# ScalarE fetches one tile of 64 row by row in pass L0 as well, and the second edge table reaches VectorE through PSUM

## What is computed

```python
h = jnp.maximum(_layernorm(x, axis=-1), 0.0)
x = x + _L0_gnn_ref(h, src, dst, edge_weight, L0_gnn_eps)       # (1+eps)*h + segment_sum(h[src]*edge_weight, dst)
h = jnp.maximum(_layernorm(x, axis=-1), 0.0)
x = x + _L1_gnn_ref(h, edge_index, edge_attr_64, edge_attr_64_n2, ...)
#   edge_weight = jnp.sum(z * edge_attr, axis=1); then 3 times:
#   agg = segment_sum(edge_weight[:, None] * (h @ conv_weight[i])[src], dst); h = gru_cell(agg, h, ...)
h = jnp.maximum(_layernorm(x, axis=-1), 0.0)
x = x + _L2_gnn_ref(h, edge_index, edge_type_16, ...)           # relation weights, attention
h = jnp.maximum(_layernorm(x, axis=-1), 0.0)
x = x + _L3_gnn_ref(h, edge_index, L3_gnn_W, L3_gnn_b)          # mean over edges, sorted by source
```

## Time and profile before

| | us |
|---|---|
| median of 3 runs | 6450.01 |
| lowest, highest | 6447.16, 6452.57 |
| profiled execution, its own time | 6448.79 |
| its span in the trace | 6446.7 |

### The profile page before, as it was taken

The page is one execution under the profiler, slowest core; times in us unless marked ns, Lnnn a source line. Parts: engine busy times, 40 slices in busy tenths (PEclk is TensorE's granted clock), DMA queues, the critical chain, the costliest instruction groups (busy, mean ns, idle before and its releaser), DMA issues.

```text
span 6446.7 us, 121607 instructions
## 1 busy us (share of the span) xinstructions
PE 3474.1 (54%) x13756; PEld 2716.5 (42%) x13756; DVE 3860.5 (60%) x14060; ACT 630.0 (10%) x1422; POOL 4692.6 (73%) x4970
## 2 busy tenths in 40 slices
PE   3444445666667555555655554695454444444444
PEld 3333334444444444554444444343343333333334
DVE  6767666666666676667677774454454444444445
ACT  1000002000001000000200000143333333000000
POOL 6777776777774677777777777675777776777775
PEclk6555556555556677667867775696555555555555
DMA  5333342222222222222222222263222222222222
GB/s 140 110 111 109 108 111 77 58 60 58 60 58 67 58 59 59 60 59 56 68 60 59 59 60 59 85 226 116 54 53 54 54 54 56 56 56 56 56 56 59
DMA packets 281533, 472.60 MB, mean 73 GB/s; under 512 B 103535, under 2 KB 178670, under 8 KB 274463
## 3 DMA queue, kind: packets, MB, share of 16 engines
q0 software_dynamic: 155024, 303.69, 18.6%
q1 hardware_dynamic: 89755, 94.70, 4.5%
q10 hardware_dynamic: 35956, 66.36, 3.0%
HBM read 379.46 MB, written 86.91 MB: 72 GB/s over the span
## 4 chain that ended last, share of the span: by engine, by line
POOL 35%; issue 20%; SPq 15%; DMA 14%; PE 10%; DVE 4%; ACT 1%; DVEq 1%; POOLq 0%; ACTq 0%
POOL G L731 34%; SPq L592 12%; DMA G<-h_rows,ix_src 10%; PE ps L835 10%; SPq L584 3%; DMA G<-h_rows 1%; DMA G<-t_rows,pos 1%; DMA t_rows<-G 1%; DVE HNA L1306 1%; PE ps L897 0%; DVEq L1295 0%; SPq L605 0%; ACT gate L1957 0%; DVE M L1286 0%; DVE bst L1223 0%
## 5 line engine op out<-in xcount | busy, mean ns | idle before, releaser
L731 POOL DMA_INDIRECT G<-h_rows,ix_src x3824 | 3632.5, 950 | 1273.9 <-issue 1017.4
L835 PE MATMUL ps<-G,M 128*128 x10000 | 2546.9, 420 | 2806.8 <-SPq L605 1904.6
L835 PEld LDWEIGHTS ps<-G,M 128*128 128x128 f32 x10000 | 2154.7, 308 | 3265.5 <-issue 3260.4
L1306 DVE TENSOR_TENSOR HNA<-HNA,ps 128x128 f32 (+1 forms) x3328 | 958.2, 288 | 1259.0 <-PE ps L835 1238.3
L1286 DVE TENSOR_SCALAR M<-irow,rel,w_l 128x128 f32<-128x128 f32 x3328 | 1205.7, 364 | 177.5 <-issue 170.7
L731 POOL DMA_INDIRECT G<-t_rows,pos x770 | 736.1, 956 | 261.3 <-issue 225.3
L1306 DVE TENSOR_TENSOR HTA<-HTA,ps 128x129 f32 x840 | 243.5, 290 | 502.0 <-PE ps L835 492.7
L835 PE MATMUL ps<-sorting 128*128 128x128 f32 x1568 | 419.1, 362 | 0.0
L1996 ACT ACTIVATE G<-G,pk 128x128 f32<-128x128 f32 x782 | 311.8, 402 | 673.0 <-DMA G<-t_rows,pos 671.7
L1306 DVE TENSOR_TENSOR X<-X,ps 128x128 f32 x832 | 239.5, 288 | 230.0 <-PE ps L835 218.0
L835 PEld LDWEIGHTS ps<-sorting 128*128 128x128 f32 x1568 | 352.6, 277 | 0.0
(11 more groups left out here) (274 smaller groups left out, 2069.8 us busy)
## 6 DMA issues: line engine op xcount, KB each, us to landing
G<-h_rows SPq DMA_DIRECT2D x7680, 0.5 KB
G<-h_rows ACTq DMA_DIRECT2D x4608, 0.5 KB
G<-h_rows,ix_src POOLq DMA_INDIRECT x3824
t_rows<-G SPq DMA_DIRECT2D x49, 1024.0 KB, 4.3
HTA<-in_edge_attr_n ACTq DMA_DIRECT2D x50, 500.0 KB
HTA<-in_edge_attr ACTq DMA_DIRECT2D x50, 500.0 KB
G<-t_rows SPq DMA_DIRECT2D x1536, 0.5 KB
G<-t_rows,pos POOLq DMA_INDIRECT x770
```

The costliest lines, as they stand in the source:

```text
L731: return nc.gpsimd.indirect_dma_start(to, None, table, bass.IndirectOffsetOnAxis(ap=ix, axis=0))
L835: return nc.tensor.matmul(dst, lhsT, rhs, start=start, stop=stop, skip_group_check=True)
L1306: V.tensor_tensor(to, to, ps[:, u % SLOTS, 0:n], ALU.add).then_inc(s_add, 1)
```

## The change

In pass L0 too, ACT fetches the 63rd tile of each 64, twelve tiles of 128 rows; POOL leaves these out. ACT does its loads of the edge tables between the rows, by a list of steps written out in the code (`edges_due`), and in the same places it copies the second table's chunk to PSUM, banks 4 and 5 or 6 and 7, two instructions of 512 columns. DVE multiplies from there: two instructions of 512 columns with one operand in SBUF and one in PSUM, where it had four of 256 with both in SBUF. It waits for ACT's copy (`s_ewp`) where it waited for the load (`s_ewl`). The semaphores of the row by row tiles are now shared by two passes each, and one wait is added in DVE's setup.

```diff
-EW_PIECE = 4
+EW_PIECE = EW_C // 2
...
-ACT_PASSES = (PASS_L1 + 1, PASS_L1 + 2, PASS_L3)
+ACT_PASSES = (PASS_L0, PASS_L1 + 1, PASS_L1 + 2, PASS_L3)
...
-        s_row = [[sem(f"s_row{k}_{q}") for q in range(2)] for k in range(3 + LAYERS)]
-        s_rowa = {k: [sem(f"s_rowa{k}_{q}") for q in range(2)] for k in ACT_PASSES}
+        s_row = [[sem(f"s_row{k}_{q}") for q in range(2)] for k in range((3 + LAYERS) // 2)]
+        s_rowa = [[sem(f"s_rowa{k}_{q}") for q in range(2)] for k in range((3 + LAYERS) // 2)]
...
             def ew_chunk(c, q, turn):
-                dve.wait_ge(s_ewl[q], 32 * (turn + 1))
-                for d in range(0, EW_C, EW_PIECE):
-                    to = za[:, q, 0, d:d + EW_PIECE, :]
-                    ins = V.tensor_tensor(to, to, za[:, q, 1, d:d + EW_PIECE, :], ALU.mult)
+                dve.wait_ge(s_ewp[q], turn + 1)
+                for h in range(2):
+                    to = za[:, q, 0, h * EW_PIECE:(h + 1) * EW_PIECE, :].rearrange("p c d -> p (c d)")
+                    ins = V.tensor_tensor(to, to, ps[0:EW_P, 4 + 2 * q + h, :], ALU.mult)
                 link(ins)
...
-            V.tensor_copy(wc[:], ps[:, 4:4 + LAYERS, 0:3 * D])
+            link(V.tensor_copy(wc[:], ps[:, 4:4 + LAYERS, 0:3 * D]))
...
+            act.wait_ge(s_ones, 16 * 2 * ROW_PARTS)
             for q in range(2):
                 ew_load(q, q)
...
-            with act.Fori(0, EW_CHUNKS // 2 - 1) as i:
-                for q in range(2):
-                    act.wait_ge(s_ewc, 2 * i + q + 1)
-                    ew_load(2 * i + 2 + q, q)
+
+            def ew_second(q, turn):
+                act.wait_ge(s_ewl[q], 32 * (turn + 1))
+                for h in range(2):
+                    ins = A.copy(ps[0:EW_P, 4 + 2 * q + h, :],
+                                 za[:, q, 1, h * EW_PIECE:(h + 1) * EW_PIECE, :].rearrange("p c d -> p (c d)"))
+                ins.then_inc(s_ewp[q], 1)
...
+            def slot_free(k, j):
+
+                act.wait_ge(s_mm, max(k * S + (j - 2) * RING + BY_ACT + BLK, 1))
+
+            loaded, copied = [2], [0]
+
+            def edges_due(step):
+                while loaded[0] < EW_CHUNKS and 16 * loaded[0] + 12 <= step:
+                    c = loaded[0]
+                    act.wait_ge(s_ewc, c - 1)
+                    ew_load(c, c % 2)
+                    loaded[0] += 1
+                while copied[0] < min(loaded[0], EW_CHUNKS) and max(16 * copied[0] + 26, 36) <= step:
+                    c = copied[0]
+                    if c == 0:
+                        act.wait_ge(s_eix, 1)
+                    ew_second(c % 2, c // 2)
+                    copied[0] += 1
+
+            for j in range(ROW_SETS * ROW_PARTS):
+                slot_free(PASS_L0, j)
+                for q in range(P // RD):
+                    rows_by_act(PASS_L0, j, q, lambda: edges_due(j * RING - 12 + 16 * q))
+                    edges_due(j * RING - 4 + 16 * q)
+            while copied[0] < EW_CHUNKS:
+                edges_due(16 * copied[0] + 26)
```

More of the change, by code:

```diff
@@ L348, in gnn_kernel @@
         s_ewl = [sem("s_ewl0"), sem("s_ewl1")]
+        s_ewp = [sem("s_ewp0"), sem("s_ewp1")]
         s_ewc = sem("s_ewc")
@@ L461, in used, with rows_before @@
             return sum(len([t for t in range(u, EF, RD) if not row_by_row(p, t)]) for p in range(k))
+        def rows_before(k, at):
+            first = [p for p in range(k - k % 2, k) if at == BY_ROW or p in ACT_PASSES]
+            return len(first) * 16 * P * ROW_SETS * ROW_PARTS // 2
         def slot_of(t):
@@ L592, in fetch @@
                     sp.dma_start(G[e:e + 1, BY_ROW + 2 * (j % 2), 0:D], table[bass.ds(row[e % RD], 1), :]) \
-                        .then_inc(s_row[k][j % 2], 16)
+                        .then_inc(s_row[k // 2][j % 2], 16)
             def arrivals(k, tiles, fetched, table, listed):
@@ L599, in one @@
                         j = t // RING
-                        here = s_row[k] if t % RING == BY_ROW else s_rowa[k]
-                        sp.wait_ge(here[j % 2], 16 * P * (c * (ROW_PARTS // 2) + j // 2 + 1))
+                        here = (s_row if t % RING == BY_ROW else s_rowa)[k // 2][j % 2]
+                        sp.wait_ge(here, rows_before(k, t % RING) + 16 * P * (c * (ROW_PARTS // 2) + j // 2 + 1))
                     else:
@@ new lines, in rows_by_act @@
+            def rows_by_act(k, j, q, between=None):
+                _, row = nc.values_load_multi_w_load_instructions(
+                    act_by_one[32 * (j % ROW_PARTS):32 * (j % ROW_PARTS) + 1, bass.ds(j // ROW_PARTS * P + q * RD, RD)],
+                    engines=[mybir.EngineType.Activation], min_val=0, max_val=NP - 1,
+                    skip_runtime_bounds_check_because="it lies in its table as every index of a gather does")
+                for e in range(RD):
+                    if between and e == RD // 2:
+                        between()
+                    act.dma_start(G[q * RD + e:q * RD + e + 1, BY_ACT + 2 * (j % 2), 0:D], h_rows[bass.ds(row[e], 1), :]) \
+                        .then_inc(s_rowa[k // 2][j % 2], 16)
@@ L1888, in part_out @@
                     .then_inc(s_part, 1)
[L1890 to L1902, removed]
             def rows_and_copies(l, v0, v1):
@@ L1992, in attend @@
                     if u == BY_ROW:
-                        act.wait_ge(s_row[PASS_L2][half], 16 * P * (i + 1))
+                        act.wait_ge(s_row[PASS_L2 // 2][half], rows_before(PASS_L2, BY_ROW) + 16 * P * (i + 1))
                     else:
```

## The result

The changed kernel takes 6465.43 us, the median of 13 runs (6457.8 to 6477.19), beside 6448.86 us for the kernel before, also 13 runs (6443.9 to 6453.28). The ratio is 1.0027, with a 95% interval of 1.0019 to 1.0034: 16.6 us slower, where 19 us less were forecast, and outside the range. The profiled execution took 6469.85 us, its span is 6468.0 us.

The account below looks back on a forecast made before the run. The prediction took POOL's gathers to bound L0. Its terms, -15.0 - 4.5 + 0 + 0.5 = -19.0 us, led from a median of 6450.01 to 6431.0 us, range 6426 to 6440.

Parts of the forecast that it names:

- the paragraph on ACT: ACT in L0: 17.2 us of work a quarter against 18.2 a chunk, so it keeps up with 1.0 us to spare.
- nothing is gained, since the pace is set behind POOL: Rival: SP has the same rows to issue, so L0 stays as it is, 6450 us; chance 0.06.
- sign for "slower": In L0 chunks come at ACT's rhythm, DVE stands before each multiply, the ring stays full and POOL waits; +50 or so.
- The slow rival: ACT sets L0's pace with quarters of up to 19.7 us, giving 6500 us; chance 0.07.
- POOL's gathers: -15.0: In L0, 12 of 770 gathers go at 1.2506 us each, all on the path that sets the end: -15.0 us.
- Two operands: -4.5: DVE's multiplies in L0 with one operand in PSUM stop lengthening POOL's gathers: -4.5 us, bounds 0 and 5.4.
- DVE: 0: Two multiplies of 512 columns take 1.3 to 1.4 us a chunk, four took 1.43; not the bound, so nothing gained.
- The start: 0, at most 2: L0's start: ACT's first copies end 1 us before DVE wants them; 0 us lost, 2 if ACT is late.
- The tail: +0.5: From L0's last gather to its last add, 7.6 us before, grows by 0 to 1.25 us; 0.5 taken.
- Later passes: What follows L0 is moved, not changed: the later passes stay unchanged to 1 us.

Follow-up runs that it names:

- e3: Changed kernel with each edge load cut into DMAs of 112 and 13 partitions instead of one of 125; 6435.41 us, ratio 0.9976 to the kernel before.
- e6: Changed kernel without the copies to PSUM (DVE multiplies from SBUF in four pieces), edge loads cut in 112 and 13 partitions; 6437.59 us, ratio 0.9985.
- e7: Kernel before with only each edge load cut in 112 and 13 partitions; 6448.51 us, ratio 1.0001.
- e1: Changed kernel without ACT's row fetch in L0, POOL gathering all 770 tiles; copies and PSUM operand stay; 6445.82 us, ratio 0.9994.
- e9: Kernel before with only each edge load cut in 124 and 1 partitions; 6449.22 us, ratio 1.0002.

## Why the prediction was wrong

**What failed.** The step is the paragraph on ACT. It priced a pair of edge loads as 0.7 us and a row as 0.40, which is what ACT spends to issue them, and nowhere asked when the data lands. "So ACT keeps up with 1.0 us to spare in each" holds for the issue (the rows of a quarter took 12.9 us at 961.11, the copies 0.59 each) and is beside the point. Its own work was even done sooner than forecast: the rows before the first copy were out at 119.4 us, not 122.4. The trace of before had 11.6 us from issue to landing for a pair, in a rhythm of 18.3 us a chunk: 63% of the time, which the prediction did not set beside SP's 84% and DVE's 70%, and the change doubled the single-row DMAs beside it. A pair then takes 20.1 us. DVE's multiplies, first to last of 50 chunks, give the pace: (1040.2 - 130.8) / 49 = 18.6 us a chunk with POOL done at 1014.7, where the plan had 18.2, and 18.0 in e3. DVE takes its chunks and its steps in one order, so the steps fall back with the chunks.

That is one of two ways in which late data reached the end. Until 628 us DVE waits for no copy, and yet from step 104 on its adds come 7 to 18 us later than before: SP stands some 10 us a turn for its own rows, and its count holds PE. From 628 us on DVE's 18 waits come on top. The runs don't tell the shares of the two.

**The dismissal.** The rival "nothing is gained, since the pace is set behind POOL" got 0.06, of it 0.02 for the DMA engines, because these were busy 0.39 of L0. That figure is a mean over 16 engines. ACT's queue alone took 15.1% of the 16, 2.4 engines' time, for what are nearly all edge loads; if that lies on 5 engines, each of these is half full with it before a row or a gather comes. In the changed kernel, packets of ACT's and SP's queues are in flight in 714 of the 800 us from 200 to 1000, where it was 473 before, and the gathers take 23% of an engine as well. If one engine has the last packets, an estimate from these rows puts it at 89 + 23%, full even if some of its packets overlap. What names the shared engine is the Trainium skill; what the runs show is that one of the engines lags, and that the time follows the shape of the loads, in the order 16, 30, 50, 64 packets, with ACT's rows (6435.4, 6436.3, 6465.4, 6541.8) and not without them (16, 50, 64: 6448.5, 6448.9, 6449.2).

**The forecast's sign for "slower".** The slow rival had part of the mechanism ("DVE stands before each multiply"), but with ACT's issue as the cause and 50 us as the price, and without SP's count. POOL hardly stopped: the ring of 64 slots let it run ahead, and the arrears came due as a tail, +25.8 us, once it had nothing left to gather.

**POOL's gathers: -15.0.** The price of a gather holds, and that POOL set the pace of the kernel before. In e6 against e7 the gathers of L0 were done in 11.2 us less and the runs 10.9 apart; the rest went into the start.

**Two operands: -4.5.** The mechanism is right, and the size somewhat high. The gathers' total fell by 3.1 us in e1 against before (770 gathers) and by 4.7 in e3 against e6 (758, 718.8 and 723.5 us), with the multiply's excess gone in both. The 4.5 lie at the upper end of that: the multiplies' part was 4.9 and went, but other gathers grew by 1.6 in e1. In the times it can't be told more closely: e1 is 5.1 us below its runs of before with an interval that includes 0.

**DVE: 0.** Two multiplies of 0.680 us, 1.36 where four took 1.43, within the 1.3 to 1.4. Right.

**The start: 0, at most 2.** Wrong, and not where the prediction looked. DVE's first multiply came at 130.8 instead of 124.6, and POOL stood 7.5 us at tile 64. But DVE did not wait for ACT's copy there; its steps were late already. The add of step 20 came at 96.3 us instead of 91.4, with PE standing for SP's count before it. From 60 to 100 us SP waited 17.0 us for POOL's gathers, 12.7 before and 12.8 in e3, so at the start the gathers landed late too. With the loads split POOL still stands 3.1 us (e3) and 3.7 (e6) at tile 64; no run separates what is left.

**The tail: +0.5.** +1.9 in e3 and +25.8 in the changed kernel. **Later passes:** unchanged, as said.

**The sum with the fault removed.** e3 has the terms as the prediction had them, apart from the DMA engine: -15.0, -3.1 to -4.7, +3.1 and +1.9 are -13.1 to -14.7, measured -15.5 (interval -23 to -8). Its 6435.4 us lie in the range that was given. So the terms on POOL were sound, and the one that was missing, the landing of the loads, was worth some 30 us.

## What to carry to other kernels

Price a DMA twice: what its issue costs the engine that starts it, and when its data lands, with whatever else uses the same DMA engines; a mean share of 16 engines (0.41 in the slow kernel, 0.47 in the fast one) does not bound the second. Before putting many one-row DMAs beside a large load, look at the load's slowest dimension, 125 here. With the rows beside it, cutting it into a multiple of 16 and a rest (112 + 13), or into 100 + 25, was worth some 30 us, and 124 + 1 cost 76; without ACT's rows no cut that was tried changed the time. When a wait is put down to a producer (ACT, here), take its wait away in an experiment before believing it: 703 us of waiting were worth nothing.

## What the hardware showed beyond that

- The same 1 MB landed in 11.6 us as two loads of 125 partitions and in 6.2 as four of 112 and 13 (e7), and in 15.5 as four of 124 and 1 (e9).
- One-row DMAs of SP became slower by what ACT issued: from 2.3 to 7.6 us, though each engine has a queue of its own.
- With POOL's gathers from 0.94 to 1.12 us beside a DVE product with two operands in SBUF, one operand in PSUM took the excess away for the gathers beside it (0.95).
- The harm sets in late and then steeply: with 30 packets of a chunk on the shared engine (counted by the Trainium skill's rule above) beside all the rows, nothing measurable was lost; 50 cost 30 us, 64 cost 106.
